# A graph layer and a routed feed-forward layer: the order of the last two nodes' steps, of the last row loads and of the last pieces, and the block without a GpSimd drain

## What is computed

```python
x = x + (segment_sum(layernorm(x)[src] * edge_weight[:, None], dst) @ W.T + b)
h = layernorm(x)                       # 12500 tokens of 256
logits = h @ gate_w + gate_b           # 8 experts; the best one is taken
idx, prb = argmax(softmax(logits)), its probability
pos = rank of the token among those of its expert
y = relu(h @ w1[idx] + b1[idx]) @ w2[idx] + b2[idx]        # 256 -> 1024 -> 256
x = x + y * prb * (pos < capacity)     # capacity 1.25 * 12500 / 8
```

## Time and profile before

| what | value |
|---|---|
| median of three runs | 2482.06 us |
| the profiled execution | 2481.74 us |
| its span | 2479.8 us |
| TensorE busy (matmuls) | 1830.4 us, 74% |
| GpSimd busy | 1789.1 us, 72% |
| VectorE, ScalarE busy | 1165.0 us, 1096.7 us |
| chain that ended last, by engine | GpSimd 60%, issue 22%, TensorE 7%, VectorE 5% |

### The profile page before, as it was taken

How to read it: one execution, slowest core, us unless ns; L and a number is a source line. 1 busy time by engine, 2 the same in 40 slices (tenths; PEclk the granted TensorE clock), 3 DMA queues, 4 the chain that set the end, 5 groups by cost and what they waited for, 6 DMA issues and landing times.

```text
span 2479.8 us, 35435 instructions
## 1 busy us (share of the span) xinstructions
PE 1830.4 (74%) x9798; PEld 1189.3 (48%) x9798; DVE 1165.0 (47%) x5806; ACT 1096.7 (44%) x2563; POOL 1789.1 (72%) x1873
## 2 busy tenths in 40 slices
PE   2334466666888898877787778777888887886797
PEld 1112233333555565544554455444555554553697
DVE  7767443334454554444444444444444444443341
ACT  6667523333454554443433444343544454443343
POOL 6677777777777677777777777777777777776661
PEclk9999975556988899887987888888988998897899
DMA  6566433335454564435445454545455455545475
GB/s 226 186 209 200 122 105 114 114 111 190 155 155 130 165 194 120 151 115 190 119 130 173 119 190 126 178 119 167 147 184 157 136 172 191 185 140 170 175 263 212
DMA packets 139884, 397.05 MB, mean 160 GB/s; under 512 B 36197, under 2 KB 62821, under 8 KB 129046
## 3 DMA queue, kind: packets, MB, share of 16 engines
q0 software_dynamic: 89712, 244.29, 33.1%
q1 hardware_dynamic: 46276, 137.66, 15.9%
q10 hardware_dynamic: 3698, 12.80, 1.4%
HBM read 498.88 MB, written 42.89 MB: 218 GB/s over the span
## 4 chain that ended last, share of the span: by engine, by line
POOL 60%; issue 22%; PE 7%; DVE 5%; ACT 4%; DMA 1%; SPq 0%; DVEq 0%; POOLq 0%; ACTq 0%
POOL msg L611 56%; POOL rows_by_expert L639 4%; ACT msg L725 3%; PE ps L970 3%; DVE wsl L1126 3%; PE ps L958 2%; PE ps L869 1%; DVE wsl L1129 1%; DMA rows_by_expert<-xrow,slot_i 1%; ACT wsl L691 0%; DMA hin<-rows_by_expert 0%; ACT pairs L734 0%; SPq L569 0%; DVE aggT L1044 0%; DVE aggT L1040 0%
## 5 line engine op out<-in xcount | busy, mean ns | idle before, releaser
L611 POOL DMA_INDIRECT msg<-normed,src_sb x1462 | 1393.7, 953 | 458.2 <-issue 445.3
L860 PE MATMUL ps<-msg,onehot 128*32 128x256 f32 x3332 | 437.1, 506 | 224.6 <-DMA msg<-normed,src_sb 200.3
L1167 DVE TENSOR_TENSOR aggT<-aggT,ps 128x192 f32 x294 | 104.7, 356 | 883.6 <-PE ps L869 858.6
L970 PE MATMUL ps<-wsl,hmid 128*128 128x256 f32 x1680 | 400.1, 393 | 1.4 <-ACT hmid L781 1.4
L734 ACT COPY pairs<-ps 128x256 f32<-128x256 f32 x294 | 111.4, 379 | 615.9 <-PE ps L860 615.1
L869 PE MATMUL ps<-shift,pairs 128*128 128x96 f32 x1176 | 237.5, 334 | 180.4 <-ACT pairs L734 180.4
L970 PEld LDWEIGHTS ps<-wsl,hmid 128*128 128x128 f32 x1680 | 322.2, 197 | 71.2 <-issue 29.2
L940 PE MATMUL ps<-wsl,hTf 128*128 128x512 f32 x680 | 353.0, 667 | 0.0
L860 PEld LDWEIGHTS ps<-msg,onehot 128*32 128x32 f32 x3332 | 139.9, 128 | 405.4 <-DMA msg<-normed,src_sb 250.7
L869 PEld LDWEIGHTS ps<-shift,pairs 128*128 128x128 f32 x1176 | 191.9, 231 | 247.1 <-ACT pairs L734 243.3
L781 ACT ACTIVATE hmid<-ps,wsl 128x128 f32<-128x128 f32 x840 | 230.6, 381 | 134.9 <-PE ps L958 70.3
(11 more groups left out here) (128 smaller groups left out, 2291.5 us busy)
## 6 DMA issues: line engine op xcount, KB each, us to landing
wsl<-in_wsecond SPq DMA_DIRECT2D x105, 1152.0 KB
wsl<-in_wfirst SPq DMA_DIRECT2D x105, 1028.0 KB
msg<-normed,src_sb POOLq DMA_INDIRECT x1462
xrow<-in_x SPq DMA_DIRECT2D x97, 128.0 KB, 2.4
wsl<-in_x SPq DMA_DIRECT2D x24, 512.0 KB, 4.2
normed<-wsl ACTq DMA_DIRECT2D x24, 512.0 KB, 3.1
hin<-rows_by_expert SPq DMA_DIRECT2D x89, 130.0 KB
msg<-in_x,src_sb POOLq DMA_INDIRECT x204
```

Of the source, the lines that this page charges most:

```text
L611: pool.indirect_dma_start(out=msg[:, m + j, :], out_offset=None, in_=x if t < RAW else ln_dram, in_offset=bass.IndirectOffsetOnAxis(ap=src ...
L860: last = nc.tensor.matmul(ps[h * QWIN:(h + 1) * QWIN, t % 2, 0:D], onehot[:, j, :], msg[:, j, :], start=i == 0, stop=i == QUARTERS[q][h] - 1)
L970: last = nc.tensor.matmul(ps[:, Y, 0:D], hmid[:, c, :], w2_at(v % 2)[:, c, :], start=c == 0, stop=c == FC - 1)
L1167: dve.tensor_tensor(columns, columns, ps[:, t % 2, D:D + KD * TWIN].rearrange("p (k c) -> p k c", k=KD), ALU.add).then_inc(s_added, 1)
```

## The change

Four things change. In the last two thirds (292 and 293) a pending piece is put ahead of the third's products instead of behind the node steps. Between the steps of the last two node tiles there is a piece at six places instead of three, `gnn 97` and `tn 96` stand behind the first of them, and `x2 97` stands behind `ra 96`. The rows of the last 16 visits are loaded behind the last full visit's rows (`("hl", full - 1) in seen`). The block is made with `no_gpsimd_drain=True`, and 14 and 12 outputs stand behind the scatters of tiles 94 and 95 instead of ten each. The list from the last third on becomes, as the code is read:

```diff
--- before.py
+++ after.py
@@ -102,6 +102,9 @@
             events.append(("raw", t + 2))
         if 0 <= t + 1 < raw:
             events.append(("rn", t + 1))
+        early = pending.pop(0) if pending and t >= thirds - 2 else None
+        if early:
+            events.append(early)
         if t >= 0:
             events.append(("mm", t))
         if moments < batches and (t + 2) * batches >= moments * (raw - 6):
@@ -130,8 +133,9 @@
             events.append(("ra", stage[3]))
         if stage[1] is not None:
             events.append(("x2", stage[1]))
-        part = pending.pop(0) if pending else None
-        if part:
+        part = early
+        if not early and pending:
+            part = pending.pop(0)
             events.append(part)
         if stage[3] is not None:
             events.append(("rk", stage[3]))
@@ -178,16 +182,22 @@
                 events.append(("z", v))
 
     assert starts[thirds - 3] == c
-    events += [("gnn", a), ("ra", c), ("rk", c), ("x2", a), ("rb", c), ("pads",), ("gnn", b), ("tn", a)]
+    events += [("gnn", a), ("ra", c), ("rk", c), ("x2", a), ("rb", c), ("pads",)]
     for t in (thirds, thirds + 1):
         for v in plan_at.get(t, ()):
             plan(v, t)
     rest()
-    events += [("lg", a), ("x2", b), ("ra", a), ("rk", a)]
+    events += [("gnn", b), ("tn", a)]
     rest()
-    events += [("rb", a), ("tn", b), ("lg", b), ("ra", b), ("rk", b)]
+    events += [("lg", a), ("ra", a), ("x2", b)]
     rest()
-    events += [("rb", b)]
+    events += [("rk", a), ("rb", a)]
+    rest()
+    events += [("tn", b)]
+    rest()
+    events += [("lg", b), ("ra", b)]
+    rest()
+    events += [("rk", b), ("rb", b)]
     planned = full
 
     def plan_last():
@@ -219,7 +229,7 @@
                     seen.add((kind, v))
                     waiting.remove(v)
         for v in list(rows):
-            if ("wb", max(v - 2, full - 1)) in seen:
+            if ("wb", max(v - 2, full - 1)) in seen and ("hl", full - 1) in seen:
                 order.append(("hl", v))
                 rows.remove(v)
     assert not first and not second and not rows
@@ -486,7 +496,7 @@
             return 16 * (v // 2 + 1)
 
         LINKS_REDO = 10
-        block = ctx.enter_context(nc.Block())
+        block = ctx.enter_context(nc.Block(no_gpsimd_drain=True))
 
         @block.sync
         def _(sp):
@@ -660,7 +670,7 @@
                     if n < NT - 4:
                         scatter(n)
             stored = 0
-            for n, first in ((NT - 4, 10), (NT - 3, 10), (NT - 2, 8), (NT - 1, V)):
+            for n, first in ((NT - 4, 14), (NT - 3, 12), (NT - 2, 8), (NT - 1, V)):
                 scatter(n)
                 while stored < V and first:
                     output(stored)
```

## The result

The changed kernel takes 2463.0 us (median of 5 runs, 2458.8 to 2467.6); the kernel before, run beside it, 2480.7 (5 runs, 2474.0 to 2483.1). The ratio is 0.9931 with an interval of 0.9915 to 0.9947, some 17 us. I had said 2461.8.

What follows compares the result with a forecast made beforehand. GpSimd's gathers bound the kernel until the last gather, then TensorE's waits in the middle, the dense tail and the final drain. 2481.74 - 9.0 (drain) - 11.0 (middle) = 2461.7, stated as 2461.8 us; range 2455.7 to 2470.

Steps and rivals of the forecast that it cites:

- No drain, 9.0 us: Kernel end: GpSimd's last DRAIN of 9.06 us is pure waiting and comes off the time, taken as 9.0 us.
- l1 84 ahead of the last products: Third 293: visit 84's first layer fits into the 6.87 us message wait, so what follows comes 3.5 us earlier.
- the 2270: Sign of an error: the forecast is wrong if the products of third 293 start later than 2270 us.
- sc 95: Scatter of node tile 95 on GpSimd, released by its route, which was to come 3.5 us earlier, at 2279.8.
- the wait for ScalarE's copy: Third 293: tile 95's logits follow its transposes at once and wait for the copy between them, 0.8 us.
- Extra outputs free by 1.8 us: GpSimd ahead of tile 95's scatter: 14 outputs instead of 10 cost nothing, done at 2278.0, route at 2279.8.
- hf 86, l2 85, hf 87, weights and rows 88 issued: Middle: rows 86 normalised 2298.6, visit 85's second layer 2300.4, rows 87 2310.2; weights issued 2317.0, rows 88 2317.7.
- Landing of rows 88: Middle, SP's queue: rows of visit 88 taken to land 6.4 us from issue, at 2324.1.
- Rows 89 hidden by 2 us: Before the tail: visit 89's rows on their way at 2327, needed at 2334; hidden by 2 us with a 5 us landing.
- The tail unchanged: Dense tail after the middle: keeps 7.24 us a visit and only begins earlier, by 11.0 us.
- the rival of a slow tail: 16 visits from 89 on at the lower clock, some 4.9 us more each, 2540 us for all; chance 3%.
- that of an idle middle: Rival: the new order in the middle gains nothing, only the drain counts, 2472.7 us; chance 7%.

Runs made afterwards that it cites:

- order_only: The changed kernel with the GpSimd drain put back, so only the order and the outputs differ from the kernel before: 2472.15 us, ratio 0.9961 to that kernel.

## Why the prediction was right, and where a size was off

- **No drain, 9.0 us:** right, 9.1 in the span and 1.8 to 1.9 us around it as before. The Trainium skill's postamble of some 5 us ("Runtime: NRT & Kernel Launch", launch sequence) has not shown itself in any run here.
- **l1 84 ahead of the last products:** right. The products started 12.0 us behind the last gather, as before (11.95), although at 2272.17 on the clock, beyond the 2270 that I had named as the sign of an error: that sign should have been counted from the gather. sc 95 came 3.8 us earlier (3.5 forecast). That the size fits is in part luck: the wait for ScalarE's copy cost 0.4 us and not 0.8, the products took 1.05 us instead of 1.91, a gain that I hadn't seen, and the short steps behind them lost 0.8 again.
- **Extra outputs free by 1.8 us:** GpSimd waited 1.81 us for the route of tile 95.
- **hf 86, l2 85, hf 87, weights and rows 88 issued:** within 0.6 us of the forecast each, as the table shows. The slow second layer of visit 85 took 6.40 us where I had 5.5 to 6.0.
- **Landing of rows 88:** this is the mis-sized term. I took 6.4 us from issue; it was 7.8 in the profiled run (1.7 us late at hf 88, 0.3 of it from the issue). The second layer behind it took 6.16 instead of 5.53. Together they are the 2.2 us at l1 88, 65.1 against 62.9. In order_only the landing was 5.7 and l1 88 came at 61.5, so the 6.4 lies between two traces of the same order.
- **Rows 89 hidden by 2 us:** right in the outcome (normalised at 2335.63, ahead of l1 88 at 2337.23), but by two misses that cancel: they were issued at 2333.17, 61.0 behind the last products instead of 58.5, and took 2.5 us instead of the 5 that I had allowed.
- **The tail unchanged:** right, 115.9 us from l1 88 to the last first layer before and after; the rival of a slow tail falls, as does that of an idle middle, which order_only refutes with its interval. (The slow tail's price in the prediction, 6.66 + 5.5 instead of 3.57 + 3.5, comes to 5.1 us a visit; the 4.9 written there is against the 7.24 between visits. Nothing hangs on it.)
- **The row loads' new condition** did nothing by itself: the order written out with and without it is the same list, because the plans of visits 89 and 90 come behind the rows of 88 anyway. What moved that issue up was the plans' new place. In the prediction I spoke of the place of the plans alone, which was right; the diff has one line that has no effect.
- **The sum:** 20.0 us forecast by its own terms, 17.7 between the medians and 17.7 in the profiled run without the 3.6 us from upstream. That the time itself, 2463.0, lies only 1.2 from my 2461.8 is in part luck: with more runs the median of the kernel before moved down from 2482.06 to 2480.70.

## What to carry to other kernels

A small load on which the next step waits should go ahead of a large load on its queue, not behind it. Rows 88 took 5.1 to 7.8 us in the four traces where the second-layer weights went just ahead of them, 2.2 to 5.9 in the three where only the first-layer weights did, the less the further ahead these had gone, and rows with nothing large just ahead 2.0 to 2.3. To issue them sooner behind the same load shortened little. Before an order is rebuilt, look at what a queue does between the wait that ends last and the transfer that answers it: the place of eight pads and one weight load (those of visits 86 and 87 were skipped by their conditions) was worth another 7.1 to 10.7 us at the last first layer, about as much as the rebuilt order (8.6 and 12.2), and stood in plain sight on SP's queue. When two profiled runs are compared, count from the last event ahead of the change, since one run can be 4 us late there for reasons of its own; and see whether the point you count from is itself behind the change, as the last products are here.

## What the runs showed that I had not expected

- GpSimd's drain behind new software DMAs costs 8.1 to 9.1 us (8.3 us in a gap; 8071 and 9059 ns where their landing had been waited for), and 46 ns when it is repeated.
- The same program took 2480 to 2481 us in three sets of runs and 2987 in one among them, with its excess in the gathers and in single waits of up to 39.66 us beside an unbroken row of GpSimd's outputs; the cause is open. The record gives the slow set and the one after it the same chip number (8), so nothing shows that it is the chip.
- Eight small transfers with addresses worked out in registers held SP's queue for 9.8 to 10.9 us (10.14 in the change, 1.27 each), ahead of rows 86 or behind them.
